# Graph layer with a mixture of experts on one core: the routing weight is applied to the hidden activations, and eight experts and the second bias accumulate in PSUM

## What is computed

```python
xn = layernorm(x)
x = x + gnn(xn, src, dst) + linear_attention(xn)      # edge softmax per source node; 8 heads
tokens = layernorm(x)
logits = tokens @ router_w.T                          # 8 experts
rw, re = top_k(softmax(logits), 2); rw = rw / rw.sum()
combine = zeros(N, 8).at[arange(N)[:, None], re].set(rw)
out = tokens
for e in range(8):                                    # every expert is computed for every token
    h = gelu(tokens @ w1[e] + b1[e])
    y = h @ w2[e] + b2[e]
    out = out + combine[:, e:e + 1] * y
x = x + out
```

## Time and profile before

| | |
|---|---|
| time, median of 3 runs (lowest, highest) | 2009.92 us (2008.76, 2011.73) |
| the profiled execution: span from first to last instruction | 2207.5 us |
| mean granted TensorE clock in it | 0.895 |
| busy in it: PE, DVE, ACT, POOL | 1718.1, 1669.8, 976.2, 994.8 us |

### The profile page before, as it was taken

The page is one execution under the profiler, slowest core; times in us unless marked ns, Lnnn a source line. Parts: engine busy times, 40 slices in busy tenths (PEclk is TensorE's granted clock), DMA queues, the critical chain, the costliest instruction groups (busy, mean ns, idle before and its releaser), DMA issues.

```text
span 2207.5 us, 40303 instructions
## 1 busy us (share of the span) xinstructions
PE 1718.1 (78%) x13588; PEld 1259.6 (57%) x13588; DVE 1669.8 (76%) x4220; ACT 976.2 (44%) x2300; POOL 994.8 (45%) x988
## 2 busy tenths in 40 slices
PE   3778785574785688888757888887888888889998
PEld 2557573463674466666535555555555555566666
DVE  5998998663566677776767887888888888886665
ACT  6322221121332233222235656666666656575655
POOL 3000003425566655655666666666666666640000
PEclk7898997796898788888968999999999999999999
DMA  5011111124554444333333333333333333860000
GB/s 174 16 59 52 51 66 32 42 84 115 145 165 130 118 120 119 102 94 90 90 90 87 86 90 83 94 83 94 82 95 92 86 92 83 89 56 11 11 20 13
DMA packets 121460, 182.21 MB, mean 83 GB/s; under 512 B 21490, under 2 KB 91902, under 8 KB 121214
## 3 DMA queue, kind: packets, MB, share of 16 engines
q0 software_dynamic: 45312, 120.06, 23.3%
q1 hardware_dynamic: 75904, 59.25, 8.6%
HBM read 152.43 MB, written 26.63 MB: 81 GB/s over the span
## 4 chain that ended last, share of the span: by engine, by line
DVE 42%; PE 23%; issue 16%; another core or an unknown queue 10%; ACT 4%; DVEq 2%; POOL 1%; DMA 0%; SPq 0%; ACTq 0%; POOLq 0%
PE bank L1255 6%; PE bank L1271 5%; DVE mloc L1615 4%; DVE big L1518 4%; DVE scr L1637 3%; DVE big L1523 3%; DVE work L1809 3%; DVE big L1520 2%; DVE big L1525 2%; DVE big L1796 2%; DVE scr L1483 2%; DVE work L1593 2%; DVE work L1610 2%; PE bank L947 1%
## 5 line engine op out<-in xcount | busy, mean ns | idle before, releaser
L664 POOL DMA_INDIRECT work<-table,tiles x904 | 921.0, 1019 | 546.6 <-PE bank L1142 277.8
L1271 PE MATMUL bank<-big 128*128 128x256 f16 x2352 | 327.7, 278 | 34.8 <-issue 34.5
L1255 PE MATMUL bank<-scr,big 128*128 128x512 f16 (+1 forms) x1248 | 282.3, 377 | 0.3 <-ACT big L871 0.3
L1140 PE MATMUL bank<-work,scr 128*128 128x257 f16 x904 | 269.9, 299 | 13.0 <-issue 10.5
L1271 PEld LDWEIGHTS bank<-big 128*128 128x128 f16 x2352 | 232.3, 99 | 78.3 <-issue 46.0
L1141 PE MATMUL bank<-work,scr 128*128 128x256 f16 x904 | 270.8, 300 | 5.9 <-issue 5.6
L1142 PE MATMUL bank<-work,scr 128*128 128x257 f16 x904 | 268.9, 297 | 5.9 <-issue 5.9
L1637 DVE SCALAR_TENSOR_TENSOR scr<-scr,gg,bank 128x257 f32<-128x257 f32 x452 | 216.7, 479 | 29.7 <-remote 16.6
L999 PE MATMUL bank<-big 128*128 128x208 f16 x1568 | 176.9, 269 | 67.7 <-DVE big L1525 60.9
L799 ACT ACTIVATE work<-bank 128x1024 f16<-128x1024 f16 x113 | 115.5, 1022 | 242.7 <-DVE mloc L1615 144.0
L999 PEld LDWEIGHTS bank<-big 128*128 128x128 f16 x1568 | 150.7, 102 | 94.6 <-issue 88.9
(11 more groups left out here) (340 smaller groups left out, 3494.1 us busy)
## 6 DMA issues: line engine op xcount, KB each, us to landing
work<-table,tiles POOLq DMA_INDIRECT x904
scr<-normed_cols SPq DMA_DIRECT2D x98, 128.0 KB
table<-big SPq DMA_DIRECT2D x49, 129.0 KB, 2.1
normed_rows<-scr SPq DMA_DIRECT2D x49, 128.5 KB, 2.6
big<-normed_rows SPq DMA_DIRECT2D x49, 128.5 KB
normed_cols<-big SPq DMA_DIRECT2D x49, 128.0 KB, 1.7
xs<-in_x_dram SPq DMA_DIRECT2D x4, 1536.0 KB, 14.2
out_dram<-work SPq DMA_DIRECT2D x48, 128.0 KB
```

Source lines behind the costliest of these rows:

```text
L664: pool.indirect_dma_start(G[:, r, j, :], None, table, bass.IndirectOffsetOnAxis(ap=col[:, t:t + 1], axis=0)).then_inc(rows_in[r // GS], 16)
L1140: pe.matmul(of[:, 0:D + 1], hi, Gh[:, r, j, 0:D + 1], start=(j == 0), stop=False)
L1255: mm = pe.matmul(bank[5 + f][:, 0:n * P], w1p[pw][:, e, h, f * P:(f + 1) * P], x2p[b % 2][px][:, h, 0:n * P], start=(h + m == 0), stop=(h ...
L1271: mm = pe.matmul(of, hTp[ph][:, k % 2, f, (j + c) * P:(j + c + 1) * P], w2p[pw][:, e, f, :], start=False, stop=(f == 1 and m == 2))
```

## The change

The routing weights are split in three float16 parts for each token (`chl`, 24 columns: high, low, high), turned by TensorE (`routing_turned`) and copied by ScalarE into `cT` (`routing_sb`). For each expert one matrix product of 512 columns with a selecting matrix (`routing_wide`) spreads that expert's weights over all 128 partitions in bank 2, which the spread of the edge loop, the transposes of the norm and the logits use too. A new instruction of VectorE (`scaled`) multiplies both halves of `hT` by them, 1024 columns, reading one operand from PSUM. Only then do `hidden_hi` and `split` follow, now one slot after `up` (`SCALE_AT`), and `down` two slots after it. `down` no longer begins a sum for each expert: banks 7 and 1 accumulate over eight experts, the second bias is one product for each tile at expert 0, and VectorE adds each half once per batch (`add`). `hT` has two buffers, `acc` one, and its first writing is moved from `norms` into `unscaled`, shortly before the add. The loading of the second bias is three small transfers in place of two.

```diff
-        DOWN_AT = {t + 1: k for t, k in UP_AT.items()}
-        ADD_AT = {t + 2: k for t, k in UP_AT.items()}
+        SCALE_AT = {t + 1: k for t, k in UP_AT.items()}
+        DOWN_AT = {t + 2: k for t, k in UP_AT.items()}
+        ADD_AT = {t + 3: b for t, (b, e) in UP_AT.items() if e == X - 1}
...
             def hidden(b, e):
                 k, n = slot(b, e), of_batch[b]
                 act.wait_ge(m_up, k + 1)
-                if k:
-                    act.wait_ge(m_lo, k)
+                if k > 1:
+                    act.wait_ge(m_lo, k - 1)
                 for f in range(2):
-                    act.activation(hT[:, f, 0:n * P], bank[5 + f][:, 0:n * P], ACT.Gelu,
+                    act.activation(hT[k % 2][:, f, 0:n * P], bank[5 + f][:, 0:n * P], ACT.Gelu,
                                    bias=b1c[:, f, e:e + 1]).then_inc(m_g, 1)
 
             def hidden_hi(b, e):
                 k, n = slot(b, e), of_batch[b]
-                act.wait_ge(m_g, 2 * k + 2)
+                act.wait_ge(m_scaled, k + 1)
                 if k > 1:
                     act.wait_ge(m_y, half_index(*divmod(k - 1, X), 0))
-                act.copy(hTp[0][:, k % 2, :, 0:n * P], hT[:, :, 0:n * P]).then_inc(m_hi, 1)
+                act.copy(hTp[0][:, k % 2, :, 0:n * P], hT[k % 2][:, :, 0:n * P]).then_inc(m_hi, 1)
...
+                if s in SCALE_AT and s - 1 not in FIRST:
+                    hidden_hi(*SCALE_AT[s])
                 if s in UP_AT:
                     hidden(*UP_AT[s])
-                    hidden_hi(*UP_AT[s])
+                if s - 1 in FIRST:
+                    routing_sb(FIRST[s - 1])
                 if s + 2 < NS:
                     one_hot_turned(s + 2)
+                if s - 1 in FIRST:
+                    hidden_hi(*SCALE_AT[s])
+                if s + 2 < NS:
...
+            def routing_turned(b, u):
+                pe.wait_ge(m_parts, b + 1)
+                pe.wait_ge(e_s3, scored(u))
+                if b:
+                    pe.wait_ge(m_scaled, slot(b, 0))
+                for j in range(of_batch[b]):
+                    mm = pe.transpose(bank[2][0:XK, :].bitcast(F16)[:, j * P:(j + 1) * P], chl[:, j, :], identh[:, :])
+                mm.then_inc(m_parts_ps, 1)
+
+            def routing_wide(b, e, u):
+                k, n = slot(b, e), of_batch[b] * P
+                pe.wait_ge(m_parts_T, b + 1)
+                pe.wait_ge(e_s3, scored(u))
+                if k:
+                    pe.wait_ge(m_scaled, k)
+                if u in FIRST:
+                    pe.wait_ge(m_lcopy, FIRST[u] + 1)
+                elif u + 1 in FIRST:
+                    pe.wait_ge(m_xlo, halves_before(FIRST[u + 1] + 1))
+                elif u + 2 in FIRST:
+                    pe.wait_ge(m_xlo, halves_before(FIRST[u + 2]) + (of_batch[FIRST[u + 2]] > 2))
+                pe.matmul(bank[2][:, 0:n], sel[:, e, :], cT[:, 0:n], start=True, stop=True).then_inc(m_wide, 1)
+
             def down(b, e, h):
-                k, i = slot(b, e), half_index(b, e, h)
+                k = slot(b, e)
                 pe.wait_ge(m_lo, k + 1)
-                if i > 1:
-                    pe.wait_ge(m_add, i - 1)
+                if b and e == 0:
+                    pe.wait_ge(m_add, halves_before(b - 1) + min(h + 1, len(halves(b - 1))))
                 j, n = halves(b)[h]
                 for c in range(n):
-                    of = bank[Y_BANK[i % 2]][:, c * D:(c + 1) * D]
-                    pe.matmul(of, onesq[:, :], b2p[:, e * D:(e + 1) * D], start=True, stop=False)
+                    of = bank[Y_BANK[h]][:, c * D:(c + 1) * D]
+                    if e == 0:
+                        pe.matmul(of, cT[:, (j + c) * P:(j + c + 1) * P], b2s, start=(c == 0), stop=False,
+                                  skip_group_check=True)
                     for f in range(2):
                         for m, (ph, pw) in enumerate(PAIRS):
                             mm = pe.matmul(of, hTp[ph][:, k % 2, f, (j + c) * P:(j + c + 1) * P], w2p[pw][:, e, f, :],
-                                           start=False, stop=(f == 1 and m == 2))
+                                           start=False, stop=(e == X - 1 and f == 1 and m == 2), skip_group_check=True)
                 mm.then_inc(m_y, 1)
...
+                if s in SCALE_AT and not near_norm(s) and s - 1 not in FIRST:
+                    routing_wide(*SCALE_AT[s], s)
                 if s + 2 < NS:
                     turn(s + 2)
+                if s in SCALE_AT and near_norm(s):
+                    routing_wide(*SCALE_AT[s], s)
+                if s - 1 in FIRST:
+                    routing_turned(FIRST[s - 1], s)
                 if 0 <= s < NS:
                     for g in range(GS * s + GS // 2, GS * (s + 1)):
                         total(g)
+                if s - 1 in FIRST:
+                    routing_wide(*SCALE_AT[s], s)
...
-                dve.tensor_tensor(comb[:, b % 2, 0:n, :], s_, wide(r_), ALU.mult).then_inc(m_comb, 1)
-                dve.wait_ge(m_comb, b + 1)
+                link(dve.tensor_tensor(comb[:, 0:n, :], s_, wide(r_), ALU.mult))
+                if b:
+                    dve.wait_ge(m_parts_ps, b)
+                c_ = comb[:, 0:n, :].rearrange("p j (a e) -> p j a e", a=1).to_broadcast([P, n, 2, X])
+                c3 = chl[:, 0:n, :].rearrange("p j (a e) -> p j a e", a=3)
+                link(dve.tensor_copy(c3[:, :, 0:3:2, :], c_))
+                dve.tensor_tensor(c3[:, :, 1, :], comb[:, 0:n, :], c3[:, :, 0, :], ALU.subtract).then_inc(m_parts, 1)
+
+            def scaled(b, e):
+                k, n = slot(b, e), of_batch[b] * P
+                dve.wait_ge(m_g, 2 * k + 2)
+                dve.wait_ge(m_wide, k + 1)
+                h_ = hT[k % 2][:, :, 0:n]
+                dve.tensor_tensor(h_, h_, bank[2][:, 0:n].rearrange("p (a n) -> p a n", a=1).to_broadcast([P, 2, n]),
+                                  ALU.mult).then_inc(m_scaled, 1)
 
             def split(b, e):
                 k, n = slot(b, e), of_batch[b]
                 dve.wait_ge(m_hi, k + 1)
-                dve.tensor_tensor(hTp[1][:, k % 2, :, 0:n * P], hT[:, :, 0:n * P], hTp[0][:, k % 2, :, 0:n * P],
+                dve.tensor_tensor(hTp[1][:, k % 2, :, 0:n * P], hT[k % 2][:, :, 0:n * P], hTp[0][:, k % 2, :, 0:n * P],
                                   ALU.subtract).then_inc(m_lo, 1)
 
-            def add(b, e, h):
-                i = half_index(b, e, h)
+            def add(b, h):
                 j, n = halves(b)[h]
-                dve.wait_ge(m_y, i + 1)
-                if e == 0:
-                    dve.wait_ge(m_acc, NB * b + of_batch[b])
-                else:
-                    dve.wait_ge(m_add, i + 1 - len(halves(b)))
-                for c in range(n):
-                    a_ = acc[b % 2][:, j + c, :]
-                    ins = dve.scalar_tensor_tensor(a_, bank[Y_BANK[i % 2]][:, c * D:(c + 1) * D], comb[:, b % 2, j + c, e:e + 1],
-                                                   a_, ALU.mult, ALU.add)
-                ins.then_inc(m_add, 1)
+                dve.wait_ge(m_y, half_index(b, X - 1, h) + 1)
+                dve.wait_ge(m_acc, NB * b + of_batch[b])
+                dve.tensor_tensor(acc[:, j:j + n, :], acc[:, j:j + n, :],
+                                  bank[Y_BANK[h]][:, 0:n * D].rearrange("p (j c) -> p j c", j=n), ALU.add
+                                  ).then_inc(m_add, 1)
 
...
+                if s - 1 in FIRST:
+                    combine(FIRST[s - 1])
+                if s in SCALE_AT and not near_norm(s) and s - 1 not in FIRST:
+                    scaled(*SCALE_AT[s])
...
-                if s in UP_AT:
-                    split(*UP_AT[s])
+                if s in SCALE_AT:
+                    split(*SCALE_AT[s])
```

134 lines of the change are left out of this document (87 added, 47 removed).

## The result

The changed kernel takes 2192.28 us (median of 4 runs, 2191.72 to 2192.86), the kernel before beside it 2009.34: a ratio of 1.0911 (95% interval 1.0896 to 1.0927), 183 us slower. Forecast were 2127 us and +117: the sign was right, the size was not, and the measured time lies just over the range (2190).

A forecast was written before the change was run, and what follows sets the result against it. Plain edge steps were taken as bound by VectorE (11.3 us), the tail by TensorE. The change closes loops of waits: 2009.9 + 38 (tail) + 79 (66 steps) = 2127 us, range 2045 to 2190.

The forecast's parts named there:

- The ring of the tail: Tail, four-tile slots: loop of waits through `up`, wide product, `scaled`, copy and gelu takes 6.70 us, +1.05 a slot.
- These now fit in its idle 1.3 us a slot ... So 2.9 for 3.6, -0.7: Tail, batch turn: transposes and logits fit TensorE's idle time; load and weight wait cost 2.9 us for 3.6.
- The last batch: Tail's one-tile batch: +0.9 us in seven slots, about 3 for its longer start and end, +9 us together.
- I take this as delay from recording many tiny products: 66 edge steps: an unexplained first-score wait, 54.6 us over the stage, is from recording and absent in plain runs.
- The ring of the steps, 12.2: 66 edge steps: loop of waits from one spread's end to the next sums to 12.2 us, taken as 12.5.
- times 66, +79: 66 edge steps: each grows by 1.2 us, from 11.3 to 12.5, +79 us in all.
- VectorE, 10.5 us of work, has slack in it, which covers `route` and the window ends: 66 edge steps: VectorE's 10.5 us fits inside the 12.5 us step, so `route` and window ends add nothing.
- What is removed and added in work: Per slot: VectorE loses 1.64 us of adds, gains `scaled` and batch work, net -0.17 us; TensorE net -0.22.
- The load of the gelu's table: ScalarE's table switch costs 1.28 us without a drain; the skill's 1.38 us drain per switch would give 2218 us.
- the third: Rival: TensorE idles more, loop clock falls from 0.93 to 0.85; steps +132, tail +15 more, 2195 us; 12%.
- Rival 1: Steps and tail: waiting loops don't bind, only saved work counts, -11 and -7 us, 1992 us; 5%.

The follow-up runs named there:

- e1: Changed kernel with ScalarE's float16 copy of the expert before put behind the next expert's gelus: 2093.52 us, ratio 1.042.
- e2: Changed kernel with the wide product ahead of `up` on TensorE in a batch's third to sixth slots: 2118.27 us, ratio 1.0533.
- e10: Changed kernel, at a tail batch's second slot the previous batch's `down` ahead of the turned weights, its adds ahead of `scaled`: 2358.63 us on a slower chip, ratio 1.0507.
- e4: Changed kernel with the next batch's norms ahead of copy and gelu on ScalarE: 2182.42 us, ratio 1.0851.
- b0_again: The kernel before, unchanged, recorded a second time: 2008.93 us, recorded span 2007.2.
- e7: Changed kernel with ScalarE order gelu, one-hot, copy; norms ahead of gelu; wide product ahead of `up`; earlier `down` and adds at tail batch turns: 2047.25 us, ratio 1.0193.
- e3: Changed kernel without the wide product and `scaled`, so routing weights are not applied: 1970.72 us, ratio 0.9808.
- e11: e7 unchanged, run again on a chip where the kernel before takes 2221.1 us: 2243.49 us, ratio 1.0098.

## Why the prediction was right in sign and wrong in size

By its own steps:

1. **The ring of the tail**: forecast 6.70 us a slot, measured 6.79. Right, and e1 and e2 cut it at two places.
2. **"These now fit in its idle 1.3 us a slot ... So 2.9 for 3.6, -0.7"**: this step failed. A whole batch was to take 48.84 + 8 x 1.05 - 0.7 = 56.5 us and takes 65.6 and 67.2. The four batches of the tail grow by 13.7, 16.8, 18.4 and 17.3 us, 66.2 together, where the forecast had 7.7 each, 28.5 for its 3.75 batches: 38 of the 46 us missed in the tail. The other 8 lie ahead of the tail's first gelu, which comes 11.4 us into it for 3.5 before; in e1 it is 3.5 again. The ledger of the batch from 2028.86 to 2096.07: eight slots of 6.79 are 54.3; the second and third slot +5.2 and +3.6, four slots with a load, transposes or a slow `up` +5.8 together, the first -1.7; sum 67.2. I counted what is new at the turn (the wait of 1.6 for the weights, the load of 1.28) as sums of work. What costs is the order: a wait of 1.87 in front of `down` puts all of `down` into the ring. e10 changes this order alone and gets 4.3 and 5.9 us a batch back, e4 1.1 and 4.3 by the norms. Part of it is clock: 4.44 for 24 products against 2.79 in a plain slot is +1.65, and `up` at 2065.93 takes 4.29 for 2.76. How order and clock share the rest is open.
3. **The last batch**: a slot of 2.55 was forecast (1.64 + 0.9), and 2.62 us measured in the plain ones. From its first gelu to its last 25.5 us for 16.1: +9.4, forecast +9. ScalarE there, answering to the earlier trace rows:

```profile
2172.01 0.62 ACT L898 ACTIVATE big<-bank,b1c 128x128 f32<-128x128 f32 x2
2174.33 0.41 ACT L906 CAST big<-big 128x256 f16<-128x256 f32 x1 [1.69 <-DVE big L1880]
2174.64 0.62 ACT L898 ACTIVATE big<-bank,b1c 128x128 f32<-128x128 f32 x2
```

4. **"I take this as delay from recording many tiny products"**: wrong (b0_again). The figure that it led to, 11.3 us for a plain step, was low by 0.3 against a mean of 11.63, so the subtraction did little harm; that is luck, since its reason was false. The reason was never tested by anything in the record, and the clock of 0.895 in it was read as this kernel's.
5. **The ring of the steps, 12.2**: its size was right, 12.1 between two gelus of plain steps. **"times 66, +79"** failed: it gives every step the loss of a plain one. Places 3 to 8 grow by 1.1 us in the mean, near the +1.2 forecast; places 1 and 2, at a batch's turn, grow by 2.9 each. The mean is 1.57 us and the sum 102. Even the hit in places 3 to 6 is in part luck, since the copy and the load, 2.3 of the 12.2 us, can leave the ring there without a gain (e1).
6. **"VectorE, 10.5 us of work, has slack in it, which covers `route` and the window ends"**: wrong. VectorE stands in order, and `scaled` waits 68.6 us for the wide product: some 30 in places 4, 5 and 7, where ready adds stand behind it, and 38 in places 8, 1 and 2. e2 takes the first part away. e1 opens ScalarE's side of the ring and gets 0.86 us a step back, e7 a further 0.30; 0.41 stays, and its cause is open.
7. **What is removed and added in work**: 692.64 to 685.96 us on VectorE, -0.10 a step for -0.17 forecast. Right, and of no weight.
8. **The load of the gelu's table**: no drain around it. Line 1292.60 of the steps takes 1.28, and the gelu starts 0.01 us behind it. The sum by the drain of the Trainium skill, "ScalarE: Activation LUTs", What ACT_TABLE_LOAD costs, 2218 us, is not what was measured; the excess over 2127 lies at the batches' turns instead, 46 us in the tail and 23 in the steps.

Of the rivals, the third came nearest with 2195 us, but its reason holds in part only. The clock of the steps is the 0.93 that I forecast with, not 0.85, though it was 0.96 before; in the tail it fell from 1.00 to 0.94 as that rival said, and it did so among others where TensorE waits at a batch's turn. That it came within 3 us is luck: it has 132 us in the steps for 102, and 53 in the tail for 84. Rival 1's gain exists, 38 us in e3, but only without the multiplication. No version run beats the kernel before with the weights applied; e7 comes within 1.9%, and within 1.0% as e11.

## What to carry to other kernels

Where engines work through their queues in order, a new producer and consumer cost what stands between them in the queues, not what they compute: write the ring down as start of one instruction to its own next start, and then write it again for each kind of slot, above all for the one where a batch turns. When a copy waits for the slowest new link, put it behind the work that the other engine waits for; here two swapped statements were worth 99 of 183 us. An experiment that moves an instruction to cover its wait must move it where the wait is: list the wait by place in the batch first. Before subtracting anything from a record that is longer than its runs, look at its clock and record the same kernel a second time.
